# Audio tower, tokens to experts: four of eight second norms and their sums on VectorE instead of GpSimd, second bias added behind the row numbers

## The reference

```python
h = patches(x) @ W.T + b                      # 960 x 1440 -> 960 x 192
h = h + attention(layernorm(h))               # within each clip
z = layernorm(h)
t = rmsnorm(z) * norm_scale
g = t @ gate_w.T + gate_b                     # 16 experts
top, idx = top_k(g, 4); w = softmax(top)
comb = sum(one_hot(idx) * w)                  # 960 x 16
y[e] = swiglu(t @ mlp1[e] + b1[e]) @ mlp2[e]
out = h + z + sum_e comb[:, e] * (y[e] + b2[e])
```

## Time and profile before

| | |
|---|---|
| median of 3 runs | 290.88 us (289.96 to 291.25) |
| the profiled execution | 291.94 us, its span 290.2 us |
| PE busy | 256.5 us, 88% of the span |
| VectorE, ScalarE, GpSimd busy | 168.7, 113.3, 172.6 us |
| chain that ended last | PE 78%, DMA 9%, GpSimd 5% |

### The profile page before, as it was taken

The page is one execution under the profiler, slowest core; times in us unless marked ns, Lnnn a source line. Parts: engine busy times, 40 slices in busy tenths (PEclk is TensorE's granted clock), DMA queues, the critical chain, the costliest instruction groups (busy, mean ns, idle before and its releaser), DMA issues.

```text
span 290.2 us, 6337 instructions
## 1 busy us (share of the span) xinstructions
PE 256.5 (88%) x1943; PEld 249.8 (86%) x1943; DVE 168.7 (58%) x425; ACT 113.3 (39%) x291; POOL 172.6 (59%) x202
## 2 busy tenths in 40 slices
PE   2899999997577079999999999999999999999980
PEld 1799999986456079999999999999999999999970
DVE  0014465567897117676676766767766667676640
ACT  1010212233142125545554555455455545554520
POOL 5013266668897412567776666767766666665752
PEclk9999999999655559999999999999999999999996
DMA  6998999999812993323423243422322333233100
GB/s 180 232 216 201 235 229 232 270 278 282 241 16 58 259 244 105 48 34 56 62 49 47 45 58 54 59 42 31 50 47 49 51 49 56 32 43 52 19 1 0
DMA packets 18589, 31.29 MB, mean 108 GB/s; under 512 B 5629, under 2 KB 12125, under 8 KB 18557
## 3 DMA queue, kind: packets, MB, share of 16 engines
q1 hardware_dynamic: 7862, 22.33, 31.2%
q0 software_dynamic: 8640, 7.76, 17.6%
q10 hardware_dynamic: 2055, 0.80, 1.1%
HBM read 26.39 MB, written 5.96 MB: 111 GB/s over the span
## 4 chain that ended last, share of the span: by engine, by line
PE 78%; DMA 9%; POOL 5%; issue 2%; DVE 2%; POOLq 1%; SPq 1%; ACT 1%; DVEq 0%
PE bank L1098 39%; PE bank L1107 14%; PE bank L905 11%; DMA hn_all<-t_rows,get_row 4%; PE bank L1080 3%; DMA x_sb<-in_x 3%; PE bank L1048 2%; PE bank L934 2%; PE bank L942 2%; DMA out<-hn_all,put_row 2%; PE bank L951 1%; POOL ln_all L429 1%; PE bank L914 1%; PE bank L1067 1%; POOL rstd L422 1%
## 5 line engine op out<-in xcount | busy, mean ns | idle before, releaser
L1098 PE MATMUL bank<-xT,x_sb 96*128 96x128 f32 (+1 forms) x1080 | 136.9, 276 | 0.8 <-ACT xT L594 0.8
L1098 PEld LDWEIGHTS bank<-xT,x_sb 96*128 96x128 f32 (+1 forms) x1080 | 131.6, 193 | 1.2 <-issue 1.2
L481 POOL DMA_INDIRECT out<-hn_all,put_row x45 | 73.0, 1622 | 52.5 <-issue 23.2
L465 POOL DMA_INDIRECT hn_all<-t_rows,get_row x45 | 47.2, 1049 | 21.0 <-issue 12.5
L1107 PE MATMUL bank<-w_sb,tokw 128*128 x270 | 51.4, 326 | 0.7 <-DVE tokw L880 0.7
L1107 PEld LDWEIGHTS bank<-w_sb,tokw 128*128 128x128 f32 x270 | 42.9, 190 | 1.0 <-issue 1.0
L869 DVE TENSOR_SCALAR ln_all<-bank 128x384 f32<-128x384 f32 x45 | 25.1, 558 | 31.4 <-PE bank L1098 31.4
L905 PE MATMUL bank<-tokw,x_sb 120*120 120x192 f32 x192 | 37.0, 353 | 6.8 <-DMA x_sb<-in_x 6.8
L611 ACT COPY x_sb<-w_sb 96x768 f32 x45 | 37.0, 823 | 12.4 <-PEq L1090 10.3
L905 PEld LDWEIGHTS bank<-tokw,x_sb 120*120 120x120 f32 x192 | 34.2, 199 | 7.8 <-DMA x_sb<-in_x 7.8
L873 DVE TENSOR_TENSOR ln_all<-ln_all 128x384 f32<-128x384 f32 x45 | 25.2, 560 | 26.5 <-ACT ln_all L630 26.5
(11 more groups left out here) (143 smaller groups left out, 229.4 us busy)
## 6 DMA issues: line engine op xcount, KB each, us to landing
w_sb<-in_w SPq DMA_DIRECT2D x16, 576.0 KB, 14.8
x_sb<-in_x SPq DMA_DIRECT2D x7, 675.0 KB, 10.9
w_sb<-in_w SPq DMA_DIRECT2D x16, 288.0 KB, 15.9
t_rows<-hn_all ACTq DMA_DIRECT2D x8, 90.0 KB, 7.9
out<-h SPq DMA_DIRECT2D x1, 720.0 KB, 6.1
hn_all<-t_rows,get_row POOLq DMA_INDIRECT x45, 3.2
out<-hn_all,put_row POOLq DMA_INDIRECT x45, 3.5
tokw<-in_tok_w SPq DMA_DIRECT2D x1, 540.0 KB, 6.7
```

The source lines that it names most:

```text
L465: g.indirect_dma_start(out=xg[slot], out_offset=None, in_=t_rows, in_offset=bass.IndirectOffsetOnAxis(ap=get_row[:, m:m + 1], axis=0),).th ...
L481: g.indirect_dma_start(out=out, out_offset=bass.IndirectOffsetOnAxis(ap=put_row[:, m:m + 1], axis=0), in_=ysb[m % RING], in_offset=None, c ...
L1098: ins = t.matmul(dst[:, m * SLOTS:(m + 1) * SLOTS], stage[0:rows, j % 2, c, o:o + 128], xT[0:rows, j % 2, c, :], start=(c == 0), stop=(c = ...
```

## The change

`add_norm2` on GpSimd is run for tiles 0 to 3 only, in the loop. For tiles 4 to 7 VectorE makes the norm and the sum behind its one-hots, `owner` and `owned`. Then it makes `get_row`, `pad_now` and `put_row`, and after them the four bias adds, which wait for four sums of GpSimd instead of eight. The one-column sigmoid writes to a column of its own, since VectorE now writes into `ln2` at that time.

```diff
+SUMS = 4
...
+        spare = sb("spare", [SLOTS, 1])
...
-                if 2 <= i < TILES:
+                if 2 <= i < SUMS + 2:
                     add_norm2(i - 2)
...
-            for i in range(TILES - 2, TILES):
-                add_norm2(i)
-
             pool.wait_ge(s_route, 1)
...
-            a.activation(sig[:, 0:1], pad_row[:, 0:1], ACT.Sigmoid)
+            a.activation(spare[:, :], pad_row[:, 0:1], ACT.Sigmoid)
...
-            dve.wait_ge(s_base, TILES)
+
+            dve.wait_ge(s_rstd2, TILES)
+            for i in range(SUMS, TILES):
+                ins = d.tensor_scalar(ln2[:, i, :], h[:, i, :], mv2[:, i, 0:1], rstd2[:, i, 0:1],
+                                      ALU.subtract, ALU.mult)
+            link(ins)
+            for i in range(SUMS, TILES):
+                ins = d.tensor_tensor(h[:, i, :], h[:, i, :], ln2[:, i, :], ALU.add)
+            link(ins)
+
+            dve.wait_ge(s_rows, 1)
+            d.tensor_copy(get_row[:, :], ps_rows[:, 0:MT]).then_inc(s_table, 1)
+
+            link(d.tensor_scalar(pad_now[:, :], ps_rows[:, MT:2 * MT], pad_row[:, 1:2], pad_row[:, 0:1],
+                                 ALU.mult, ALU.add))
+            d.tensor_tensor(put_row[:, :], pad_now[:, :], ps_rows[:, 0:MT], ALU.add).then_inc(s_table, 1)
+            dve.wait_ge(s_base, SUMS)
             for q in range(4):
                 dve.wait_ge(s_b2, q + 1)
                 d.tensor_tensor(h[:, 2 * q:2 * q + 2, :], h[:, 2 * q:2 * q + 2, :], ps_b2[q],
                                 ALU.add).then_inc(s_b2c, 1)
 
-            dve.wait_ge(s_rows, 1)
-            d.tensor_copy(get_row[:, :], ps_rows[:, 0:MT]).then_inc(s_table, 1)
-
-            link(d.tensor_scalar(pad_now[:, :], ps_rows[:, MT:2 * MT], pad_row[:, 1:2], pad_row[:, 0:1],
-                                 ALU.mult, ALU.add))
-            d.tensor_tensor(put_row[:, :], pad_now[:, :], ps_rows[:, 0:MT], ALU.add).then_inc(s_table, 1)
 
             dve.wait_ge(s_owner, 2)
```

## The result

The changed kernel is slower: 293.68 us (median of 20 runs) against 291.32 for the kernel before on the same chip, a ratio of 1.0082 [1.006, 1.0103], or about 2.4 us. The profiled execution took 291.99 us with a span of 290.2. That is one of its quickest, and 0.05 us more than the one of before; what the chip usually pays has to come from more than this pair.

The account below looks back on a forecast made before the run. The bridge to the PE-bound expert tiles bounds the kernel, the gather last by about 2 us. With staging taking over, the first product moves from 103.84 to 104.75, +0.9 us on 290.88: 291.8 us, range 289.2 to 293.2.

Parts of the forecast that it names:

- Step (1): GpSimd without norms and sums of tiles 4 to 7: route weights start at 79.2, row numbers 0.55 us earlier.
- Step (2): VectorE behind its one-hots: four norms and sums take 2.5 us, end at 91.4, covered by PE with 0.8 us spare.
- third rival: Slower: VectorE's sums and GpSimd's one-hots exclude each other between 88.9 and 93 us; 293.0 at the bound; chance 0.22.
- Step (3): Bias adds behind put_row: gather lands near 96 instead of 102.25, but base store and SyncE's issues come 3.67 us later.
- second rival: Faster: the stalls in SyncE's store and load issues vanish, -1.75 us, 289.1; chance 0.12.
- first rival: No net change: SyncE's issue stretch shrinks by about 1 us, staging ready when the gather was; 290.9; chance 0.13.
- the +0.35: SyncE's nine issues behind the fourth bias add take 0.35 us longer; bounds -2.3 and +1.1.
- the sum: First product starts at the later of gather (about 97.5) and staging (104.75), against 103.84: +0.9 us.

Follow-up runs that it names:

- the repeat: The kernel before, unchanged, run once more against runs of the kernel before on the same chip: 291.91 us, ratio 1.0006.

## Why the prediction was right and where it was wrong

The direction and the new limit were the forecast ones: SyncE's queue takes over from the gather. The size was short: 2.4 us measured against 0.9 forecast, and the measured time lies 0.5 us above the range. Of the 1.9 us between the forecast 291.8 and 293.68, 0.44 is the kernel before itself, 291.32 in 20 runs against 290.88 in the three that the forecast started from.

Step (1) held: route weights at 79.26 against 79.2, the cast 0.17 us. Row numbers came 0.42 us earlier, not 0.55.

Step (2) held: the eight instructions end at 91.54 (forecast 91.4), covered by 0.8 us. The third rival's mechanism is there in part: the one-hots took 8.96 us instead of 7.96. But VectorE and PE had room for that 1 us, and get_row didn't wait for either, so the slower kernel came by another cause. The Trainium skill, page SBUF — State Buffer, section Who interferes with whom, has the exclusion for VectorE instructions with two SBUF inputs, which the sums are. This trace agrees with it only for the last one-hot, 0.92 us instead of 0.60 beside the sums; the larger loss, 1.26 instead of 0.60, fell beside the norms, which have one SBUF tensor and two columns as scalars, and the one-hot between them took 0.60 beside the first sum.

Step (3): the early gather held (issued at 92.88, landed 3.0 us later). So did the store 3.8 us later and SyncE's count as the new limit. Neither stall vanished (second rival): 1.66 and 1.73 us again, and 1.65 to 1.79 in every kernel that has loads behind the store. The nine issues took 7.42 us, 0.13 less than before: not the 1 us less of the first rival, and the +0.35 that I added for longer ones was wrong.

The step that failed is the sum, and in it the premise that whatever moves the first product moves the end by as much. Three terms of it:

- From the staging copy to the first product I took 1.2 us; it was 105.06 - 103.23 = 1.83. I had PE's transposes beside the staging copy; they stand behind PE's second check of the count and start 0.37 us after the copy does. Between the xT copy's end and the product lie another 0.41 us, in which PE's queue ends its read of `owner` for the third slot; they stood in the chain of before too, and I left them out. With the shorter issues the product came 0.3 us later than forecast.
- The kernel before was taken from one trace. Its product started at 103.84 there, at 103.22 in the repeat. Against the mean of two the delay is 1.9 us, not 0.9. The gather's landing varies (102.25 and 101.63); where SyncE's queue sets the start, an early gather brings nothing.
- The clock. That a product started 1 to 2 us later can meet the full clock 3 us later stood in no term (107.46 for a product at 103.22, 111.34 for one at 105.60); it is worth 0.6 to 1.2 us in the executions that show it, most of the changed kernel's.

In an execution with the late clock, 1.9 us and some 0.7 are 2.6; 2.4 were measured. What stays open: how much of the 2.4 us is the clock's in the mean of executions; why the start of the route weights, and with it the bridge, shifts by 0.3 us between executions; why the clock came back early in the profiled changed execution; and the tail, where a scatter of 4.4 us instead of 3.5 stands ahead of a wait of PE's of 0.42 us in the first trace of before (262 to 274 us).

## What to carry to other kernels

Before something is moved in an in-order queue, list what stands behind it and who waits for the last of that: here a count that was ready long before stood behind a store and eight loads, and became the bound as soon as the gather in front of it was gone. Look up the second-last releaser and the spread of the last one over more than one execution, since the margin of 1.9 us in one trace was 1.6 in the next (gather at 101.63, weights staged at 99.99). A reordering that loses may be half of one that wins: with the count freed and the load tail halved, the same order gave 1.2%.

## What the runs showed of the hardware

- In the two traces of each kernel and the one with late bias adds alone, the full TensorE clock came back 3.6 to 6.2 us after the first product, at 107.5, 108.3, 108.6, 111.9 or 111.3, while PE had no gap. With 13 idle products behind the row products it rose to 1.00 and fell again while PE paused: windows of that kernel (columns as above).

```profile
96.00:100.00 4.00, 0.00 (x0) 0.00 (x0) 0.45 (x1) 0.00 (x0) 2.24 (x3) 1.00 0.74 176
...
102.00:106.00 4.00, 4.00 (x19) 3.98 (x20) 0.57 (x2) 0.74 (x3) 1.12 (x2) 0.50 0.27 61
```

- Idle products alone made the kernel before 0.4% faster.
- One read of `owner` by PE's queue took 0.31 to 0.35 us in the two kernels, and 1.12 to 1.33 us in the two of the new order with the early count, beside SyncE's load issues.
- Behind queued weight loads a store of 60 KB landed after 14.4 to 15.1 us instead of 2.3, a scatter after 8.13 instead of 3.5 (median), a gather, behind the base store too, after 8.95 instead of 3.2 (median).
